# Splitting each adding transfer of a mixture-of-experts decoder layer into two transfers of 64 rows

## The reference, cut to what matters

```python
xd = jnp.zeros((E, CAP + 1, D), x.dtype).at[e_flat, slot].set(x[tok])
h = _relu2(jnp.einsum('ecd,eid->eci', xd, w1))
yd = jnp.einsum('eci,edi->ecd', h, w2)
gate = w.reshape(-1)[:, None] * keep[:, None].astype(x.dtype)
y_assign = yd[e_flat, slot] * gate
routed = jnp.zeros((T, D), x.dtype).at[tok].add(y_assign)
...
shared = _relu2(x @ shared_up_w.T) @ shared_down_w.T
x = x + (shared + routed)
```

## Time and profile before

| | |
|---|---|
| time, median of 3 runs | 989.93 us (986.37 to 991.56) |
| time of the profiled execution | 993.13 us |
| its span, first to last instruction | 991.3 us |
| first adding transfer issued | 579.78 us from the span's start |
| last adding transfer issued | 984.99 us |
| mean granted clock of TensorE | 0.961 |

### The profile page before, as it was taken

The page is one execution under the profiler, slowest core; times in us unless marked ns, Lnnn a source line. Parts: engine busy times, 40 slices in busy tenths (PEclk is TensorE's granted clock), DMA queues, the critical chain, the costliest instruction groups (busy, mean ns, idle before and its releaser), DMA issues. The chain is left out here.

```text
span 991.3 us, 14544 instructions
## 1 busy us (share of the span) xinstructions
PE 893.3 (90%) x4913; PEld 627.6 (63%) x4913; DVE 551.9 (56%) x1143; ACT 232.5 (23%) x716; POOL 464.1 (47%) x512
## 2 busy tenths in 40 slices
PE   4799999988899999869999999999999799898980
PEld 3566666664677777766444486867676567575840
DVE  4788888867688888886889422323222222131220
ACT  1465656461400000113110021111121111111200
POOL 1644452533588888630183323554454454444422
PEclk9989999999999999979999999999999899899995
DMA  7300000020533333033006558898988889889853
GB/s 291 112 1 2 1 2 1 2 75 1 199 112 96 97 99 95 0 118 138 0 1 226 187 162 259 258 273 236 276 264 237 221 252 277 269 227 278 267 122 53
DMA packets 44125, 143.40 MB, mean 145 GB/s; under 512 B 7280, under 2 KB 11632, under 8 KB 35120
## 3 DMA queue, kind: packets, MB, share of 16 engines
q1 hardware_dynamic: 26352, 96.46, 26.4%
q0 software_dynamic: 14912, 37.76, 19.3%
q10 hardware_dynamic: 2816, 8.59, 2.3%
HBM read 114.36 MB, written 28.43 MB: 144 GB/s over the span
## 5 line engine op out<-in xcount | busy, mean ns | idle before, releaser
L1359 PE MATMUL ps<-arena 128*128 128x128 f32 (+4 forms) x2128 | 521.4, 403 | 11.6 <-DVE arena L813 5.7
L1359 PEld LDWEIGHTS ps<-arena 128*128 128x128 f32 x2128 | 342.2, 193 | 154.0 <-issue 107.6
L596 POOL DMA_INDIRECT out<-arena,scatter_rows x64 | 102.0, 1594 | 216.7 <-DMA out<-arena,scatter_rows 147.2
L1294 DVE TENSOR_TENSOR arena<-arena 128x256 f32<-128x256 f32 x64 | 27.4, 427 | 222.1 <-ACT arena L798 215.9
L1359 PE MATMUL ps<-features_T,arena 128*128 (+2 forms) x640 | 116.0, 338 | 0.0
L646 ACT ACTIVATE arena<-ps 128x512 f32<-128x512 f32 (+1 forms) x137 | 78.4, 591 | 129.0 <-DVE residual L1258 56.8
L1359 PEld LDWEIGHTS ps<-features_T,arena 128*128 128x128 f32 x640 | 84.7, 188 | 37.3 <-issue 37.3
L468 POOL TENSOR_TENSOR arena<-arena 128x512 f32<-128x512 f32 x48 | 49.2, 1057 | 87.4 <-DVE arena L833 87.4
L585 POOL DMA_INDIRECT arena<-token_rows,gather_rows x64 | 66.3, 1037 | 38.2 <-DVE gather_rows L1287 27.1
L798 ACT ACTIVATE arena<-ps 128x256 f32<-128x256 f32 x64 | 24.5, 383 | 248.8 <-PE ps L1359 247.1
L656 ACT ACTIVATE arena<-arena 128x128 f32<-128x128 f32 x192 | 74.0, 389 | 16.6 <-DVE arena L821 16.3
(11 more groups left out here) (174 smaller groups left out, 1069.3 us busy)
## 6 DMA issues: line engine op xcount, KB each, us to landing
arena<-wexp SPq DMA_DIRECT2D x48, 1024.0 KB
residual<-wexp SPq DMA_DIRECT2D x16, 1024.0 KB
arena<-toeplitz_rows SPq DMA_DIRECT2D x32, 256.0 KB, 3.1
arena<-ctxE SPq DMA_DIRECT2D x32, 192.0 KB, 3.2
residual<-x SPq DMA_DIRECT2D x4, 1024.0 KB, 5.4
token_rows<-arena SPq DMA_DIRECT2D x16, 256.0 KB, 2.0
arena<-suT ACTq DMA_DIRECT2D x1, 2048.0 KB, 7.7
arena<-sdT ACTq DMA_DIRECT2D x1, 2048.0 KB, 12.6
```

Source lines behind the costliest of these rows:

```text
L596: pool.indirect_dma_start(out, bass.IndirectOffsetOnAxis(ap=idxs[:, s % NY:s % NY + 1], axis=0), ysb[:, s % NY, :], None, compute_op=ALU.a ...
L1359: ins = TE.matmul(out_ap, lhsT, rhs, start=(n == 0), stop=(n == len(pairs) - 1))
```

## The change

Each adding transfer of 128 slots becomes two of 64 slots (partitions 0 to 63 and 64 to 127), issued one behind the other in the same link. Both stand behind one wait for the landing of the link before; each adds 16 to `added`, so all counts double. [...] The mark and the gather stand behind the second transfer.

```diff
-        idxs = sb("scatter_rows", [P, 4], u32)
-        idxt = sb("tile_scatter_rows", [P, 1], u32)
-        tile_rows = sb("tile_rows", [P, NT // 4])
+        idxh = sb("slot_rows_by_halves", [P // 2, E, 2], u32)
+        idxs = sb("scatter_rows", [P // 2, 4, 2], u32)
+        idxt = sb("tile_scatter_rows", [P // 2, 2], u32)
+        tile_rows = sb("tile_rows", [P // 2, NT // 4, 2])
...
-            G.iota(tile_rows[:], [[P, NT // 4]], base=T // 4, channel_multiplier=1, allow_small_or_imprecise_dtypes=True)
+            G.iota(tile_rows[:], [[P, NT // 4], [P // 2, 2]], base=T // 4, channel_multiplier=1,
+                   allow_small_or_imprecise_dtypes=True)
...
-                pool.indirect_dma_start(out, bass.IndirectOffsetOnAxis(ap=idxs[:, s % NY:s % NY + 1], axis=0),
-                                        ysb[:, s % NY, :], None, compute_op=ALU.add).then_inc(added, 16)
+                for h, slots in enumerate((slice(0, P // 2), slice(P // 2, P))):
+                    pool.indirect_dma_start(out, bass.IndirectOffsetOnAxis(ap=idxs[:, s % NY, h:h + 1], axis=0),
+                                            ysb[slots, s % NY, :], None, compute_op=ALU.add).then_inc(added, 16)
...
-                pool.wait_ge(added, j * (16 * LINKS) + 16 * (GROUP - 1))
+                pool.wait_ge(added, j * (32 * LINKS) + 32 * (GROUP - 1))
...
-                                        bass.IndirectOffsetOnAxis(ap=idxt[:, 0:1], axis=0),
-                                        ytile.rearrange("p g d -> p (g d)"), None, compute_op=ALU.add)\
-                    .then_inc(added, 16)
+                for h, pairs in enumerate((slice(0, P // 2), slice(P // 2, P))):
+                    pool.indirect_dma_start(out.rearrange("(r g) d -> r (g d)", g=2),
+                                            bass.IndirectOffsetOnAxis(ap=idxt[:, h:h + 1], axis=0),
+                                            ytile[pairs].rearrange("p g d -> p (g d)"), None, compute_op=ALU.add)\
+                        .then_inc(added, 16)
...
+            for h in range(2):
+                V.tensor_copy(idxh[:, :, h], idxU[h * (P // 2):(h + 1) * (P // 2), 0:E])
+            V.drain()
...
-                    V.tensor_copy(idxs[:, s % NY:s % NY + 1], idxU[:, ds(i * UE + s, 1)])
+                    V.tensor_copy(idxs[:, s % NY, :], idxh[:, ds(i * UE + s, 1), :].rearrange("p e h -> p (e h)"))
```

More of the change, by code:

```diff
@@ L427, in _ @@
                     load_expert(s, i)
-            sp.wait_ge(added, 16 * (E + NT // 4))
+            sp.wait_ge(added, 32 * (E + NT // 4))
         @block.gpsimd
@@ L604, in scatter_tiles @@
                 pool.wait_ge(tile_ready, j + 2)
-                pool.wait_ge(added, j * (16 * LINKS) + 16 * (GROUP - 1))
+                pool.wait_ge(added, j * (32 * LINKS) + 32 * (GROUP - 1))
                 pool.sem_inc(scatter_landed, 1)
-                pool.indirect_dma_start(out.rearrange("(r g) d -> r (g d)", g=2),
-                                        bass.IndirectOffsetOnAxis(ap=idxt[:, 0:1], axis=0),
-                                        ytile.rearrange("p g d -> p (g d)"), None, compute_op=ALU.add)\
-                    .then_inc(added, 16)
+                for h, pairs in enumerate((slice(0, P // 2), slice(P // 2, P))):
[3 more added lines that the diff above has]
+                        .then_inc(added, 16)
             last = E // GROUP - 1
@@ L625, in group @@
                     if n < GROUP:
-                        scatter(n % UE, j * 2 + n // UE, j * (16 * LINKS) + 16 * (n if n < GROUP - 1 else n + 1))
+                        scatter(n % UE, j * 2 + n // UE, j * (32 * LINKS) + 32 * (n if n < GROUP - 1 else n + 1))
                     elif more:
-                        scatter(0, j * 2 + 2, j * (16 * LINKS) + 16 * LINKS)
+                        scatter(0, j * 2 + 2, j * (32 * LINKS) + 32 * LINKS)
                     if more or r < UE:
@@ L1311, in experts @@
                         if g == 1:
-                            V.tensor_copy(idxt[:], tile_rows[:, ds(j, 1)])
+                            V.tensor_copy(idxt[:], tile_rows[:, ds(j, 1), :].rearrange("p j h -> p (j h)"))
                             V.drain().then_inc(tile_ready, 1)
```

## The result

The changed kernel took 1069.72 us at the median (1067.95 to 1071.50, 4 runs), the one before in the same session 990.74 (986.37 to 1002.47, 4 runs): a ratio of 1.076 with a 95% interval of 1.072 to 1.081. The ratio compares fast executions alone; the two medians give 1.080. The direction was forecast, the size was not: +22 us were predicted, some +79 measured, above the range's end of 1062. The profiled execution of the changed kernel took 1069.02 us, 75.9 more than that of before (993.13).

A forecast was written before the change was run, and what follows sets the result against it. POOL's chain of adding transfers was taken as the bound: +0.19 us per quiet link and +0.15 for later releases made +0.34 over 64 links, +22 us. The median was forecast at 1012 us, range 970 to 1062.

The forecast's parts named there:

- What bounds the kernel: POOL's chain of adding transfers, each awaiting the previous landing; a longer link lengthens the kernel one for one over 64 links.
- The writing, h = 1.04: On POOL, writing the descriptors of a 64-slot adding transfer takes 1.04 us, as a gather of 128 rows does.
- The bound from below (0.78): On POOL, a 64-slot add's writing takes 0.78 us if all of it goes by rows.
- the bound from above: On POOL, a 64-slot add's writing takes 1.56 us if none of it goes by rows.
- The rest of a link, 3.29: From the end of the second half's writing to the next issue: 3.92 less 0.63 for half the bytes, 3.29 us.
- Lateness: 0.8 us at 0.15 a link: Mark, weights and gather come 0.8 us later in a link and meet the next add, costing 0.15 us per link.
- B: Follow-up theory, not in the original prediction: halves suffer because new weights start before both are through; 1090 us or more.
- Tables: Extra index copies on DVE, mostly hidden under POOL's wait before the first link: at most 0.3 us in all.
- The writing hardly shrinks with the rows: Rival: a 64-slot add's writing on POOL takes 1.3 to 1.56 us; kernel 1035 to 1069 us; chance 0.16.
- The serial queue: Rival: the second transfer's bytes wait in the DMA queues until the first lands; +2.1 us a link, 1127 us; chance 0.06.
- Faster: Rival: halves overlap in a pipeline, saving 0.33 us or more a link, and might escape weight-delayed landings; 965 to 985; chance 0.25.
- No change: Rival: later releases cost nothing and a 64-slot writing takes near 0.95 us; within 5 us of 990; chance 0.13.

The follow-up runs named there:

- a half alone: Kernel before the change, adding only slots 0 to 63 of each expert and leaving out the other rows: 970.03 us, ratio 0.978.
- the wide mark: Kernel before the change, with the mark's instruction widened from 128x1 to 128x780 numbers, so weights and gather are released later: 1026.31 us, ratio 1.037.
- the quarters: Changed kernel with four adding transfers of 32 slots per expert instead of two of 64, the tiles' link keeping two: 1181.34 us, ratio 1.195.

## Why the prediction was wrong

**What bounds the kernel** held. The chain of links ended last before and after, and a longer link lengthened the kernel one for one.

**The writing, h = 1.04**, is the step that failed. The working took the 0.5 to 0.6 us between an add and a gather of as many rows as the price of 128 further descriptors, and so made 64 slots of an add cost what 128 of a gather do. An h above 1.3 was among its own signs of being wrong. Measured were 1.58, 1.41 and 1.30 us for 128, 64 and 32 slots: 64 slots are 0.17 us, 32 are 0.11, and some 1.2 us are fixed (an estimate, from the line through these three). The difference to the gather is mostly not one of rows. The bound from below (0.78) lay far off, and the bound from above, taken from the fact that bytes don't count, was near. The line drawn from the Trainium skill ("DMA: Bandwidth & Descriptors", Anatomy of one DMA), that descriptor generation is small and grows only after many descriptors, fits these three numbers in how little they grow; "small" it isn't on this chain, where 1.41 us of a link of 6.11 are one writing. The 0.5 us that I set against it should not have outweighed it.

**The rest of a link, 3.29**, was right in kind: 2.99, with 3.05 for a half alone. The second half finds nothing of the first in its way, and saves no start either: 2.99 is just under the 3 that was to be the sign of that, but a half with nothing ahead of it does as well. The term was 0.3 too long because it took bytes alone as the measure of a half; half the bytes in half the rows save 0.9. With h = 1.41 and the measured rest the quiet link is 2.82 + 0.30 + 2.99 = 6.11, which is what the timeline shows; +0.63 instead of +0.19, 42 us instead of 13.

**Lateness: 0.8 us at 0.15 a link** was mis-sized twice. The mark is 1.56 later, since it stands behind the whole second writing; and the part of a link above the quiet one grows by about 0.36, not 0.15, some 24 us. Shown is that this part comes with the weights: where they are taken away, the link stays 0.2 above the quiet one in both kernels. Shown too is that lateness can be enough for it: with whole adds, marks that end at 3.14 and 3.09 us instead of 1.80 cost 0.38 a link (the gather ahead of the mark) and 0.45 (gather and weights late). How much of the 0.36 it is in the changed kernel isn't shown. Its link is longer, so from the gather, with which the weights start, to the next link's first add it is 2.59 us by the quiet link (6.11 - 3.52), where the wide mark leaves 2.22 (5.48 - 3.26); the run with the mark between the halves went B's way, and the quarters have a still later mark and pay 0.1. The bounds (0 and 0.8) held the value; the choice near the low end rested on the add's bytes getting longer alone, which did not give enough. The pattern is open as well. Without the tiles' links and the first, the changed kernel has 15 links that are 1.9 us or more above its quiet one (10 in the run with the last add whole), the kernel before 5; the two with whole adds and late weights have 5 and 7, and pay in many smaller delays. In which queue an add waits for the weights was not measured.

**Tables**: 0.3 us at most were allowed. The first link came 4.0 us later, but in the kernels with the same tables it was issued at 580.04 and 581.36, and in those without them between 579.78 and 587.38. So the spread between executions is wider than the 4.0, and no part of it is shown to be the change's.

**The rivals.** *The writing hardly shrinks with the rows* (chance 0.16) is what happened; its own arithmetic at h = 1.41 gives 6.41 + 0.15 - 5.48 = +1.08 a link, +69 us and 1059 with the forecast's 0.15 for the lateness, which its 1035 to 1069 left out. The measured 1069.7 lies just above that range: what was missing is the rest of the lateness, the first link and the end of the program, less the 0.3 by which the time behind the writing was put too long. *The serial queue* is refuted: behind the second half's writing the next issue comes after 2.99 us, where a half with nothing ahead of it has 3.05, and a further transfer of the quarters lengthens the link by 1.27 us, not by 3.3 and more. The rule that halves of the partitions aren't worth splitting (the Trainium skill, "DMA: Bandwidth & Descriptors", Rules for kernel authors) came out right here, but its reason, that they serialize, isn't what costs in a quiet link here: a half alone saves 0.9 us behind the writing, and the fixed writing of the second eats it. *Faster* needed h below 0.945. Its second leg, halves that escape the weights, went the other way: links 1.9 us or more above the quiet one rose from 5 to 15. *No change* needed h near 0.95 and a free lateness, and had neither.

**The end of the program** had no term at all. It is 5.6 us of the 75.9, and 4.8 of them lie behind the last landing (SP's wait of 6.4 for 1.6). Their cause is open.

In sum, for the profiled executions: 42 for the quiet link, which is the writing, 24 for what the load adds, 4 for the first link, 5.6 at the end. The forecast had +22 for all of it: of its +0.34 a link 0.19 was the quiet link, measured 0.63, and 0.15 the lateness, measured 0.36.

## What to carry to other kernels

Before an indirect DMA on a serial chain is split, measure the writing of one with fewer rows: here the fixed part was 1.2 of 1.58 us (an estimate), so each further transfer adds 1.6 to 1.7 us of writing and pause, and only what is saved elsewhere in the link can pay for it; halves saved 1.1. An instruction that releases other traffic has a place, not just a time: releasing the weights 1.3 us later behind a whole add cost 3.5% here, and releasing them 1.7 us earlier in the changed kernel, ahead of the second half, 15%. A sum of waits that falls (147.2 to 101.1 us) says little when the same engine writes more; compare the period of the chain.

## What the runs showed that was not expected

- The writing of an adding indirect DMA went little by its rows: 1.58, 1.41 and 1.30 us for 128, 64 and 32 slots of 2 KB, 1.41 also for 64 slots of 4 KB.
- Releasing 1024 KB of weights ahead of the second half of an add makes its link some 3.4 us longer (9.48 at the mean, for 6.11 quiet), while four adds of 32 slots with the weights behind them pay 0.1 us for the same weights.
- A drain on POOL behind an adding transfer left POOL idle for 2.88 us, about until it had landed; a drain with nothing in flight took 0.21.
- POOL's closing drain ends 1.0 to 2.7 us behind SP's last landing with one adding transfer a link, 3.9 with quarters and 6.1 to 6.4 with halves throughout. It was 1.2 where the loop has drains of its own. Why was not found.
